# A fused attention and sparse-FFN kernel: x's split copy on ScalarE, the context's on GpSimd, P and out in one PSUM bank, and the attention phase unrolled

## The chip, the core and the metric

The kernel runs on one core of a Trainium2 chip. TensorE is called PE here, VectorE DVE, ScalarE ACT, GpSimd POOL and SyncE SP, as in the profile. The metric is the time of one execution on the device in microseconds (us), of which the median over several runs is taken. The profile comes from one more execution, recorded by the hardware profiler.

## The reference

The input x is (32, 64, 512), the context ctx (32, 64, 512). In the first half each of the 32 samples goes through a cross attention with linear cost, in the second all 2048 rows go through a sparse FFN:

```python
q = layernorm(x)                       # over the 512 columns
qh, kh, vh = Wq @ q, Wk @ ctx, Wv @ ctx        # 8 heads of 64, per sample
qh = softmax(qh, over the 64 rows of a head) / 8
kh = softmax(kh, over the 512 columns)
context = einsum('hdn,hen->hde', kh, vh)
out = Wo @ einsum('hde,hdn->hen', context, qh) + bo
x = x + out / norm(out) * g * 8
...
h = relu(x_ln @ w1.T) where it is the largest of its 32 by a rank-16 forecast, else 0
x = x + h @ w2t
```

The order of the products is changed in the kernel: with P = ctx E^T (64x512, E the exponentials of kh, not yet divided by their sums) and vo = Wv^T Wo^T per head (computed once), G = P^T vo, scaled by the sums, is the matrix that the softmaxed Q is multiplied with. So Wv and Wo cost little per sample.

## The kernel before

**Two phases.** `attention_phase` handles one sample per tile, 32 tiles, and writes the attention's output to a scratch tensor in HBM. `ffn_phase` then handles 16 tiles of two samples. The change touches the first phase alone.

**The pipeline.** Each engine has its own program, a sequence of steps g = -1 to 33, and the engines meet through semaphores alone; nothing plans the order but the order in which the lines stand. In step g three samples are in work at once: sample g+1 is prepared (layernorm, splits), sample g gets its K projection and later its Q projection, the E of sample g-1 is turned and multiplied with the context (P), and for sample g-2 Q is turned and multiplied with G (out). The condition `real(known, s)` says whether sample g+s exists. `steps` writes out the steps g = -1 to 4 and 29 to 33 and runs the 24 steps between in a loop of 12 rounds of two, in which the waits are for register values.

**The splits.** The two projections need more precision than one product in fp32r gives. Each input is loaded twice, into partitions 0 to 63 and 64 to 127. A copy rounds all 128 partitions to fp32r (x_split: DVE L352; c_split: ACT L411), and then POOL replaces the lower 64 by the remainder, value minus rounded value (x_split L247, c_split L251). A matmul over 128 partitions so sums the rounded part and the remainder. `x_ready` and `c_ready` count the finished splits; PE's projections wait for them (L507, L490), and SP waits for them before it loads the tile after next (L184, L186).

**PE's step** (L434 to L514): turn(0), that is four 128x128 transposes of E into turn_e and four of Q into turn_q; the 16 records of the G matmuls (L483), which need the copy of P from the step before; turn(1); products(0), which wait for G of DVE; the K projection; turn(2), products(1), turn(3), products(2), products(3); the Q projection. products(m) is one matmul of P (L471, PSUM bank pg, partitions 0 to 63) and one of out (L474, bank acc, partitions 64 to 127). turn_q waits for q_scaled, that is for POOL's L236.

**DVE's step** (L287 to L354): for each half of Q the maximum over a head (qmax) and the subtraction (L310), with G (L293) behind the first half; neg_kmax of the K projection, twice (L323); bn_stats and bn_aggr of x (L327, L329); twice the sum of Q's exponentials and its reciprocal (L333, L339); krec; the normalized x (xn, L347); its rounded copy (L352). In step 1 `split_ffn_constants` (L270) follows, on raw constants that lie in out_sb and Q.

**ACT's step** (L360 to L422): the copies of turn_e and turn_q to SBUF (ET, QT) and the exponentials in turn, then c_split's rounded copy (L411), the eviction of P (L414) and that of out with the bias bo (L421).

**POOL's step** (L209 to L253): the split of a slice of the FFN weights, 448 columns (L218, L220), which waits for c_ready; var_eps and rstd (L226, L229), which wait for the moments; the two multiplications of Q by its reciprocal sums (L236); the lower halves of x_split (L247) and c_split (L251).

## Time and profile before

| what | us |
|---|---|
| median of three runs (lowest, highest) | 937.48 (936.69, 938.23) |
| span of the profiled execution, first to last instruction | 936.1 |
| time of an execution around that span, median less span | 1.4 |
| PE busy | 845.2 (90%) |
| DVE busy | 723.7 (77%) |
| POOL busy | 426.4 (46%) |
| ACT busy | 404.7 (43%) |

The attention phase takes the span up to about 500 us, the FFN the rest. The shares are means over both phases, which load the engines differently, so the phase must be read by itself. The mean granted clock of TensorE over the span is 0.980 of full speed. A time in a timeline is a start, counted from the span's start, and the number behind it is how long the instruction (or the group, as x4 says) took; in brackets stands how long the engine had been idle before it and what ended that. Consecutive instructions of an engine overlap by some hundredths, so that a start to a start is the better measure of what one costs.

### The profile page before, as it was taken

How to read it: one execution, taken by the hardware profiler on the slowest of the kernel's cores; microseconds unless marked ns; L12 is line 12 of the kernel's file. 1: busy time of each engine (PE TensorE's matmuls, PEld its weight loads, DVE VectorE, ACT ScalarE, POOL GpSimd, SP SyncE). 2: the span in 40 equal slices, each digit the busy share in tenths (PEclk: the TensorE clock that was granted, in tenths of full speed). 3: DMA queues.
4: the chain of work that ended last, by engine and by line, in shares of the span. 5: the costliest groups of instructions: out<-in, count | busy, mean ns of one | idle time of the engine just before them, and what ended most of it. 6: DMA issues, size and time to landing. Idle time of an engine off the chain costs nothing. (4 is left out here: it accounts for less than half of the span.)

```text
span 936.1 us, 15499 instructions
## 1 busy us (share of the span) xinstructions
PE 845.2 (90%) x4752; PEld 599.4 (64%) x4752; DVE 723.7 (77%) x1020; ACT 404.7 (43%) x802; POOL 426.4 (46%) x422
## 2 busy tenths in 40 slices
PE   3679989899999899999994999999999999999998
PEld 2445555554555555555552788888888888888887
DVE  3989999999999999999971566666667666666664
ACT  2457777677777776776772111111111111111110
POOL 2635575665665755656640333333233333333322
PEclk9979999999999999999996799999999999999999
DMA  7212322312222222223002010110001010110000
GB/s 206 71 32 62 84 63 69 85 55 76 78 61 79 68 68 81 55 76 87 24 7 79 1 35 34 35 35 12 22 34 34 34 34 34 34 34 34 11 0 23
DMA packets 30200, 47.71 MB, mean 51 GB/s; under 512 B 4832, under 2 KB 13152, under 8 KB 30176
## 3 DMA queue, kind: packets, MB, share of 16 engines
q1 hardware_dynamic: 30176, 47.40, 17.3%
q8 instruction: 13, 0.21, 0.1%
q14 instruction: 11, 0.09, 0.0%
HBM read 39.00 MB, written 8.39 MB: 51 GB/s over the span
## 5 line engine op out<-in xcount | busy, mean ns | idle before, releaser
L471 PE MATMUL pg<-ET,ctxT 128*64 128x512 f32 x256 | 136.5, 616 | 40.9 <-DVE G L293 39.1
L626 POOL TENSOR_TENSOR ranked<-mask,rank 128x512 bf16<-128x512 bf16 x64 | 70.0, 1094 | 157.3 <-DVE mask L764 156.3
L236 POOL TENSOR_TENSOR Q<-Q,qrec 128x1024 f32<-128x1024 f32 x64 | 125.9, 1988 | 30.6 <-DVE qrec L339 30.6
L474 PE MATMUL acc<-QT,G 128*64 128x512 f32 x256 | 137.7, 621 | 0.0
L368 ACT ACTIVATE Q<-Q 128x1024 f32<-128x1024 f32 x64 | 67.8, 1059 | 74.1 <-DVE Q L310 74.1
L689 ACT ACTIVATE hT_hi<-turned 128x512 fp32r<-128x512 f32 x64 | 34.9, 545 | 149.4 <-PE turned L900 149.4
L390 ACT ACTIVATE ET<-turn_e 128x512 f32<-128x512 f32 x128 | 76.4, 597 | 49.9 <-PE turn_e L444 49.9
L890 PE MATMUL hidden<-weights_hi,xT_hi 128*128 128x512 f32 (+1 forms) x256 | 96.0, 375 | 0.0
L890 PE MATMUL hidden<-weights_hi,xT_lo 128*128 128x512 f32 (+1 forms) x256 | 94.8, 370 | 0.0
L890 PE MATMUL hidden<-weights_lo,xT_hi 128*128 128x512 f32 (+1 forms) x256 | 94.6, 370 | 0.0
L379 ACT ACTIVATE E<-slot,neg_kmax 128x512 f32<-128x512 f32 x128 | 88.0, 710 | 12.9 <-DVE neg_kmax L323 12.9
L913 PE MATMUL acc<-weights_hi,hT_hi 128*128 128x512 f32 x224 | 92.5, 413 | 0.0
L913 PE MATMUL acc<-weights_hi,hT_lo 128*128 128x512 f32 x224 | 88.0, 393 | 0.0
L913 PE MATMUL acc<-weights_lo,hT_hi 128*128 128x512 f32 x224 | 87.6, 391 | 0.0
L323 DVE TENSOR_REDUCE neg_kmax<-slot 128x2 f32<-128x1024 f32 x64 | 77.0, 1224 | 11.2 <-PE slot L498 8.1
L783 DVE SCALAR_TENSOR_TENSOR h_sb<-behind,hidden 128x512 f32<-128x512 bf16 x64 | 39.7, 621 | 58.0 <-POOL behind L635 36.4
L444 PEld LDWEIGHTS turn_e<-ident,E 128*128 128x128 f32 x512 | 59.1, 141 | 39.4 <-ACT ET L390 28.4
L452 PE MATMUL turn_q<-ident,Q 128*128 128x128 f32 x512 | 78.6, 276 | 5.8 <-POOL Q L236 4.4
L444 PE MATMUL turn_e<-ident,E 128*128 128x128 f32 x512 | 80.9, 281 | 1.2 <-ACT ET L390 1.2
L310 DVE TENSOR_TENSOR Q<-slot,qmax 128x1024 f32<-128x1024 f32 x64 | 78.3, 1224 | 4.5
L396 ACT ACTIVATE QT<-turn_q 128x512 f32<-128x512 f32 x128 | 76.8, 600 | 8.5 <-PE turn_q L452 6.5
L471 PEld LDWEIGHTS pg<-ET,ctxT 128*64 128x64 f32 x256 | 24.6, 135 | 85.6 <-issue 56.4
(96 smaller groups left out, 1894.3 us busy)
## 6 DMA issues: line engine op xcount, KB each, us to landing
x_in<-in_x SPq DMA_DIRECT2D x64, 128.0 KB, 2.6
c_in<-in_ctx SPq DMA_DIRECT2D x64, 128.0 KB, 2.7
stage<-in_ffn_w SPq DMA_DIRECT2D x32, 224.0 KB, 2.5
ctxT<-in_ctxT SPq DMA_DIRECT2D x32, 128.0 KB, 2.1
attn_out<-out_sb SPq DMA_DIRECT2D x32, 128.0 KB, 2.3
attn<-attn_out SPq DMA_DIRECT2D x16, 256.0 KB, 2.7
xr<-in_x SPq DMA_DIRECT2D x16, 256.0 KB, 2.9
out<-result SPq DMA_DIRECT2D x16, 256.0 KB, 2.0
```

What stands on the lines that cost most here:

```text
L236: nc.gpsimd.tensor_tensor(half, half, qrec[1 - par][:, s, :].unsqueeze(2).broadcast_to([P, HALF, D]), ALU.mult).then_inc(q_scaled, 1)
L310: nc.vector.tensor_tensor(heads(Q[1 - par][:, 2 * s:2 * s + 2, :]), src, qmax[:, s, :].unsqueeze(2).broadcast_to([P, HALF, D]), ALU.subtra ...
L323: nc.vector.tensor_reduce(neg_kmax[par][:, 2 * s:2 * s + 2], slot[s][:], AX.X, ALU.max, negate=True).then_inc(k_max, 1)
L379: last = nc.scalar.activation(E[par][:, j, :], slot[s][:, i, :], ACT.Exp, bias=neg_kmax[par][:, j:j + 1], accum_out=ksum[par][:, j:j + 1])
L390: nc.scalar.activation(ET[m % 2][:], turn_e[:], ACT.Copy).then_inc(e_copied, 1)
L396: nc.scalar.activation(QT[m % 2][:], turn_q[:], ACT.Copy).then_inc(q_copied, 1)
L444: last = nc.tensor.transpose(turn_e[:, j * P:(j + 1) * P], E[1 - par][:, j, m * P:(m + 1) * P], ident[:])
L452: last = nc.tensor.transpose(turn_q[:, t * P:(t + 1) * P], Q[par][:, t, m * P:(m + 1) * P], ident[:])
L471: nc.tensor.matmul(pg[0:C, :], ctxT[1 - par][:, m, :], ET[m % 2][:], start=(m == 0), stop=(m == NT - 1)).then_inc(p_mm, 1)
L474: nc.tensor.matmul(acc[C:P, :], G[par][:, m, :], QT[m % 2][:], start=(m == 0), stop=(m == HT - 1)).then_inc(out_mm, 1)
L890: last = nc.tensor.matmul(hidden[c % 2][:, 0:w], x[par][:, m, :], wt, start=(n == 0), stop=(n == len(terms) - 1))
L913: last = nc.tensor.matmul(acc[:], h[c % 2][:, cols], w2(wt, kt), start=(kt == 0 and n == 0), stop=(kt == KT - 1 and n == 2))
```

## The change

Four things change in the attention phase:

- DVE no longer makes the rounded copy of x. ACT does, as its last instruction of a step.
- ACT no longer makes the rounded copy of the context. POOL does, and its lower half follows at once; both now stand between rstd and the multiplications of Q, which wait for them (`c_ready`). x's lower half stays behind those multiplications.
- P and out go into one PSUM bank, po (P in partitions 0 to 63, out in 64 to 127), and one ACT instruction evicts both with a bias that is zero for P. G's matmuls use the other bank, gp. The raw FFN constants that lay in out_sb now lie in QT.
- The loop of 12 rounds is written out; all waits are for constants.

The diff, cut to what matters (renamings of tiles and semaphores left out):

```diff
--- before.py
+++ after.py
@@ -42,7 +42,6 @@
...
-FIRST_LOOPED, LAST_LOOPED = 5, B - 4
...
-def steps(eng, step):
-
-    for g in range(-1, FIRST_LOOPED):
-        step(g, g // 2, g % 2, g)
-    with eng.Fori(FIRST_LOOPED // 2, LAST_LOOPED // 2) as k:
-        step(2 * k + 1, k, 1, None)
-        step(2 * k + 2, k + 1, 0, None)
-    for g in range(LAST_LOOPED + 1, B + 2):
+def steps(step):
+
+    for g in range(-1, B + 2):
         step(g, g // 2, g % 2, g)
...
         ET = [sb(f"ET{i}", [P, HID]) for i in range(2)]
         QT = [sb(f"QT{i}", [P, N]) for i in range(2)]
-        PT = sb("PT", [C, HID])
         G = [sb(f"G{i}", [P, HT, C]) for i in range(2)]
-        out_sb = [sb(f"out_sb{i}", [P, N]) for i in range(2)]
-        c1_raw, rank_raw = out_sb[0][:], out_sb[1][:]
+        po_sb = [sb(f"po_sb{i}", [P, N]) for i in range(2)]
+        c1_raw, rank_raw = QT[0][:], QT[1][:]
...
-        pg = ps("pg", [P, 512])
-        acc = ps("acc", [P, 512])
+        po = ps("po", [P, 512])
+        gp = ps("gp", [P, 512])
...
@@ -193,10 +186,10 @@
                             sp.wait_ge(p_mm, NT * g)
                         load_ctxT(g + 1, 1 - par)
                     if real(known, -2):
-                        sp.wait_ge(out_copied, g - 1)
-                        sp.dma_start(scratch[g - 2], out_sb[par][C:P, :]).then_inc(stored[par], 16)
-
-                steps(sp, step)
+                        sp.wait_ge(po_copied, g)
+                        sp.dma_start(scratch[g - 2], po_sb[par][C:P, :]).then_inc(stored[par], 16)
+
+                steps(step)
...
             def _(pool):
                 nc.gpsimd.memset(neg_half[:], -0.5).then_inc(powers_set, 1)
                 nc.gpsimd.memset(eps[:], EPS).then_inc(powers_set, 1)
-                pool.wait_ge(powers_set, 2)
+                nc.gpsimd.memset(po_bias[0:C, :], 0.0).then_inc(powers_set, 1)
+                pool.wait_ge(powers_set, 3)
 
                 def step(g, k, par, known):
 
 
                     if later(g + 1 if known is None else min(g + 1, B)):
                         pool.wait_ge(c_ready, g + 1 if known is None else min(g + 1, B))
+                        pool.wait_ge(x_ready, g + 1 if known is None else min(g + 1, B))
...
@@ -228,8 +223,19 @@
                         pool.wait_ge(x_var, g + 2)
                         nc.gpsimd.tensor_tensor(rstd[1 - par][:], var_eps[:], neg_half[:],
                                                 ALU.pow).then_inc(x_rstd, 1)
+
+                        pool.wait_ge(c_loaded[1 - par], 32 * ((k if par == 0 else k + 1) + 1))
+                        if later(2 * g):
+                            pool.wait_ge(k_proj, 2 * g)
+                        nc.gpsimd.tensor_copy(c_split[1 - par][:], c_in[1 - par][:]).then_inc(c_hi, 1)
+                        pool.wait_ge(c_hi, g + 2)
+                        nc.gpsimd.tensor_tensor(c_split[1 - par][C:P, :], c_in[1 - par][C:P, :],
+                                                c_split[1 - par][C:P, :].bitcast(fp32),
+                                                ALU.subtract).then_inc(c_ready, 1)
                     if real(known, -1):
 
+                        if real(known, 1):
+                            pool.wait_ge(c_ready, g + 2)
                         for s in range(2):
                             pool.wait_ge(q_rec, 2 * g - 1 + s)
                             half = heads(Q[1 - par][:, 2 * s:2 * s + 2, :])
@@ -247,12 +253,8 @@
                         nc.gpsimd.tensor_tensor(x_split[1 - par][C:P, :], xn[C:P, :],
                                                 x_split[1 - par][C:P, :].bitcast(fp32),
                                                 ALU.subtract).then_inc(x_ready, 1)
-                        pool.wait_ge(c_hi, g + 2)
-                        nc.gpsimd.tensor_tensor(c_split[1 - par][C:P, :], c_in[1 - par][C:P, :],
-                                                c_split[1 - par][C:P, :].bitcast(fp32),
-                                                ALU.subtract).then_inc(c_ready, 1)
-
-                steps(pool, step)
+
+                steps(step)
...
@@ -346,14 +348,10 @@
                             dve.wait_ge(x_ready, g + 1)
                         nc.vector.tensor_scalar(xn[:], x_in[1 - par][:], moments[1 - par][:, 0:1],
                                                 rstd[1 - par][:], ALU.subtract, ALU.mult).then_inc(x_normed, 1)
-                        dve.wait_ge(x_normed, g + 2)
-                        if later(2 * g):
-                            dve.wait_ge(q_proj, 2 * g)
-                        nc.vector.tensor_copy(x_split[1 - par][:], xn[:]).then_inc(x_hi, 1)
                     if known == 1:
                         split_ffn_constants()
 
-                steps(dve, step)
+                steps(step)
...
@@ -390,6 +388,8 @@
                             nc.scalar.activation(ET[m % 2][:], turn_e[:], ACT.Copy).then_inc(e_copied, 1)
                         if real(known, -2):
                             use = HT * (g - 2) + m
+                            if known == 2 and m == 0:
+                                act.wait_ge(ffn_consts_done, 5)
                             act.wait_ge(q_turned, use + 1)
                             if later(use - 1):
                                 act.wait_ge(out_mm, use - 1)
...
@@ -403,31 +403,32 @@
                     exp_k(0)
                     copy(3)
                     exp_k(1)
+                    if real(known, -1) or real(known, -2):
+
+                        rows = slice(0 if real(known, -1) else C, P if real(known, -2) else C)
+                        if known == 1:
+                            act.wait_ge(powers_set, 3)
+                        if real(known, -1):
+                            act.wait_ge(p_mm, NT * g)
+                        if real(known, -2):
+                            act.wait_ge(out_mm, HT * (g - 1))
+                            if later(16 * (k - 1)):
+                                act.wait_ge(stored[par], 16 * (k - 1))
+                        nc.scalar.activation(po_sb[par][rows, :], po[rows, :], ACT.Identity,
+                                             bias=po_bias[rows, :]).then_inc(po_copied, 1)
                     if real(known, 1):
-
-                        act.wait_ge(c_loaded[1 - par], 32 * ((k if par == 0 else k + 1) + 1))
+                        act.wait_ge(x_normed, g + 2)
                         if later(2 * g):
-                            act.wait_ge(k_proj, 2 * g)
-                        nc.scalar.activation(c_split[1 - par][:], c_in[1 - par][:], ACT.Copy).then_inc(c_hi, 1)
-                    if real(known, -1):
-                        act.wait_ge(p_mm, NT * g)
-                        nc.scalar.activation(PT[:], pg[0:C, :], ACT.Copy).then_inc(p_copied, 1)
-                    if real(known, -2):
-                        if known == 2:
-                            act.wait_ge(ffn_consts_done, 5)
-                        act.wait_ge(out_mm, HT * (g - 1))
-                        if later(16 * (k - 1)):
-                            act.wait_ge(stored[par], 16 * (k - 1))
-                        nc.scalar.activation(out_sb[par][C:P, :], acc[C:P, :], ACT.Identity,
-                                             bias=bo[C:P, :]).then_inc(out_copied, 1)
-
-                steps(act, step)
+                            act.wait_ge(q_proj, 2 * g)
+                        nc.scalar.activation(x_split[1 - par][:], xn[:], ACT.Copy).then_inc(x_hi, 1)
+
+                steps(step)
...
@@ -459,29 +460,27 @@
                             pe.wait_ge(e_copied, NT * (g - 1) + m + 1)
                             if m == 0:
                                 pe.wait_ge(ctxT_loaded[1 - par], 16 * ((k - 1 if par == 0 else k) + 1))
-                                if later(g - 1):
-                                    pe.wait_ge(g_ready, g - 1)
                         if real(known, -2):
                             pe.wait_ge(q_copied, HT * (g - 2) + m + 1)
                             if m == 0:
                                 pe.wait_ge(g_ready, g - 1)
-                                if later(g - 2):
-                                    pe.wait_ge(out_copied, g - 2)
                         if real(known, -1):
-                            nc.tensor.matmul(pg[0:C, :], ctxT[1 - par][:, m, :], ET[m % 2][:],
+                            nc.tensor.matmul(po[0:C, :], ctxT[1 - par][:, m, :], ET[m % 2][:],
                                              start=(m == 0), stop=(m == NT - 1)).then_inc(p_mm, 1)
                         if real(known, -2):
-                            nc.tensor.matmul(acc[C:P, :], G[par][:, m, :], QT[m % 2][:],
+                            nc.tensor.matmul(po[C:P, :], G[par][:, m, :], QT[m % 2][:],
                                              start=(m == 0), stop=(m == HT - 1)).then_inc(out_mm, 1)
 
                     turn(0)
                     if real(known, -2):
                         pe.wait_ge(vo_ready, 1)
-                        pe.wait_ge(p_copied, g - 1)
+                        pe.wait_ge(po_copied, g - 1)
+                        if later(g - 2):
+                            pe.wait_ge(g_ready, g - 2)
                         for h in range(HEADS):
                             r = (h % 2) * D
-                            last = nc.tensor.matmul(pg[r:r + D, (h // 2) * C:(h // 2 + 1) * C],
-                                                    PT[:, h * D:(h + 1) * D], vo[:, h, :], start=True, stop=True)
+                            last = nc.tensor.matmul(gp[r:r + D, (h // 2) * C:(h // 2 + 1) * C],
+                                                    po_sb[1 - par][0:C, h * D:(h + 1) * D], vo[:, h, :], start=True, stop=True)
                         last.then_inc(g_mm, 1)
                     turn(1)
```

## Rows read from the trace of the kernel before

**Rows 1.** Windows view, 300 to 400 us: busy us (instructions) by engine, clock, DMA, GB/s.
```profile
300.00:400.00 100.00, 91.67 (x560) 53.70 (x558) 96.37 (x112) 74.34 (x147) 62.15 (x56) 1.00 0.25 70
```

**Rows 2.** Timeline of DVE, one step in the loop: start us, us, engine, line, operation.
```profile
302.84 0.18 DVE L329 BATCH_NORM_AGGREGATE moments<-stats 128x2 f32<-128x6 f32 x1
...
306.80 2.01 DVE L352 CAST x_split<-xn 128x512 fp32r<-128x512 f32 x1
...
317.20 0.18 DVE L329 BATCH_NORM_AGGREGATE moments<-stats 128x2 f32<-128x6 f32 x1
```

**Rows 3.** Timeline of DVE in unrolled steps, the first and the last.
```profile
59.18 0.18 DVE L329 BATCH_NORM_AGGREGATE moments<-stats 128x2 f32<-128x6 f32 x1
...
457.45 2.41 DVE L323 TENSOR_REDUCE neg_kmax<-slot 128x2 f32<-128x1024 f32 x2
...
460.55 0.18 DVE L329 BATCH_NORM_AGGREGATE moments<-stats 128x2 f32<-128x6 f32 x1
...
463.44 0.94 DVE L347 TENSOR_SCALAR xn<-x_in,moments,rstd 128x512 f32<-128x512 f32 x1
...
471.64 2.42 DVE L323 TENSOR_REDUCE neg_kmax<-slot 128x2 f32<-128x1024 f32 x2
```

**Rows 4.** Timeline of PE, 455 to 506 us, the same unrolled steps.
```profile
466.29 0.63 PE L452 MATMUL turn_q<-ident,Q 128*128 128x128 f32 x4
466.85 0.68 PE L483 MATMUL pg<-vo,PT 64*64 64x64 f32 x16
467.46 0.66 PE L444 MATMUL turn_e<-ident,E 128*128 128x128 f32 x4
467.96 0.60 PE L452 MATMUL turn_q<-ident,Q 128*128 128x128 f32 x4
469.40 0.61 PE L471 MATMUL pg<-ET,ctxT 128*64 128x512 f32 x1 [0.85 <-DVE G L293]
469.41 0.64 PE L474 MATMUL acc<-QT,G 128*64 128x512 f32 x1
469.86 0.59 PE L471 MATMUL pg<-ET,ctxT 128*64 128x512 f32 x1
```

**Rows 5.** Timelines of the start: DVE, POOL and PE.
```profile
13.66 0.43 DVE L352 CAST x_split<-xn 128x512 fp32r<-128x512 f32 x1
...
15.45 1.26 POOL L251 TENSOR_TENSOR c_split<-c_in,c_split 64x512 fp32r<-64x512 f32 x1
...
16.77 0.79 PE L497 MATMUL slot<-c_split,wk_hi 128*128 128x512 f32 x1 [6.38 <-POOL c_split L251]
```

**Rows 6.** Timeline of POOL, 455 to 500 us (unrolled steps).
```profile
460.81 0.19 POOL L226 TENSOR_TENSOR var_eps<-moments,eps 128x1 f32<-128x1 f32 x1 [4.07 <-DVE moments L329]
461.08 0.55 POOL L229 TENSOR_TENSOR rstd<-var_eps,neg_half 128x1 f32<-128x1 f32 x1
462.20 3.95 POOL L236 TENSOR_TENSOR Q<-Q,qrec 128x1024 f32<-128x1024 f32 x2 [0.57 <-DVE qrec L339]
466.60 1.26 POOL L247 TENSOR_TENSOR x_split<-xn,x_split 64x512 fp32r<-64x512 f32 x1 [0.45 <-DVE x_split L352]
467.82 1.27 POOL L251 TENSOR_TENSOR c_split<-c_in,c_split 64x512 fp32r<-64x512 f32 x1
469.16 0.56 POOL L218 CAST weights_hi<-stage 128x448 fp32r<-128x448 f32 x1
469.80 1.14 POOL L220 TENSOR_TENSOR weights_lo<-stage,weights_hi 128x448 fp32r<-128x448 f32 x1
475.55 3.76 POOL L236 TENSOR_TENSOR Q<-Q,qrec 128x1024 f32<-128x1024 f32 x2 [4.61 <-DVE qrec L339]
```

**Rows 7.** All instructions of line 218: ns minimum, median, maximum, first and last start.
```profile
L218 POOL CAST weights_hi<-stage x32: 556/556/635, 16.8 to 469.2; 128x448 f32 x24, 128x448 fp32r<-128x448 f32 x8
```

**Rows 8.** Groups of instructions, 100 to 500 us, on ACT: busy us, mean ns | idle before.
```profile
L421 ACT ACTIVATE out_sb<-acc,bo 64x512 f32<-64x512 f32 x29 | 19.8, 684 | 2.0 <-PE acc L474 1.3
L411 ACT ACTIVATE c_split<-c_in 128x512 fp32r<-128x512 f32 x26 | 17.7, 681 | 0.0
```

More of the change, by code:

```diff
@@ L79, in attention_phase @@
         vo = sb("vo", [C, HEADS, C])
-        bo = sb("bo", [P, 1])
+        po_bias = sb("po_bias", [P, 1])
         ident = shared["ident"]
@@ L135, in attention_phase @@
         q_sum, q_rec, q_scaled = sem("q_sum"), sem("q_rec"), sem("q_scaled")
-        e_turned, e_copied, p_mm, p_copied = sem("e_turned"), sem("e_copied"), sem("p_mm"), sem("p_copied")
-        q_turned, q_copied, out_mm, out_copied = sem("q_turned"), sem("q_copied"), sem("out_mm"), sem("out_copied")
+        e_turned, e_copied, p_mm, po_copied = sem("e_turned"), sem("e_copied"), sem("p_mm"), sem("po_copied")
+        q_turned, q_copied, out_mm = sem("q_turned"), sem("q_copied"), sem("out_mm")
         g_mm, g_ready = sem("g_mm"), sem("g_ready")
@@ L167, in _ @@
                 sp.dma_start(woT, A["woT"]).then_inc(consts_in, 16)
-                sp.dma_start(bo[C:P, :], A["bo"]).then_inc(consts_in, 16)
+                sp.dma_start(po_bias[C:P, :], A["bo"]).then_inc(consts_in, 16)
                 sp.dma_start(ident[:], A["ident"]).then_inc(consts_in, 16)
@@ L266, in prologue @@
                     dve.wait_ge(vo_mm, 1)
-                    nc.vector.tensor_copy(vo[:], acc[0:C, :].rearrange("c (h o) -> c h o", h=HEADS))\
+                    nc.vector.tensor_copy(vo[:], gp[0:C, :].rearrange("c (h o) -> c h o", h=HEADS))\
                         .then_inc(vo_ready, 1)
@@ L293, in gains @@
                             nc.vector.scalar_tensor_tensor(
-                                G[par][:], pg[:, 0:HT * C].rearrange("p (j o) -> p j o", j=HT), SCALE,
+                                G[par][:], gp[:, 0:HT * C].rearrange("p (j o) -> p j o", j=HT), SCALE,
                                 krec[:].unsqueeze(2).broadcast_to([P, HT, C]), ALU.mult, ALU.mult)\
@@ L429, in _ @@
                 for h in range(HEADS):
-                    last = nc.tensor.matmul(acc[0:C, h * C:(h + 1) * C], wv[:, h, :], woT[:, h, :],
+                    last = nc.tensor.matmul(gp[0:C, h * C:(h + 1) * C], wv[:, h, :], woT[:, h, :],
                                             start=True, stop=True)
@@ L514, in step @@
                             last.then_inc(q_proj, 1)
-                steps(pe, step)
+                steps(step)
 def ffn_phase(nc, A, shared, scratch, out):
```

## The prediction

> **What bounds the kernel now.** I read the page's shares first, then the windows by stage, then the timelines of DVE, PE and POOL for single steps. In the attention phase DVE is busy 96.4 of 100 us and PE 91.7 [rows 1]. Let A be the start of the moments instruction (L329), one per step. In the loop A comes back after 317.20 - 302.84 = 14.36 us [rows 2]; in the last unrolled step I get 471.64 - 457.45 = 14.19 from one neg_kmax to the next [rows 3]. From A at 59.18 to A at 460.55 there are 28 such intervals, 401.4 us, 14.33 each [rows 3]. DVE is the bound, and PE waits for it once a step, 0.85 us in front of L471, for G [rows 4]. The reader should see two more things.
>
> First, the removed cast L352 is not 2.01 us of work. At the start, where POOL is idle, it takes 0.43 us [rows 5], in a step 2.01 us [rows 2], because it is held while POOL runs its two Q multiplications (L236). POOL pays too: the two took 3.95 us with DVE's xn (L347, 463.44) among them, and 3.76 us at 475.55, where there is no xn [rows 3, 6].
>
> Second, a chain through POOL is hardly shorter than the step: A at 460.55, var_eps, rstd, Q multiplications to 462.20 + 3.95 = 466.15, turn_q(0) on PE at 466.29 [rows 3, 4, 6]. PE is released there by POOL and only then meets the wait for G. What enters that chain before L236 is paid as soon as it exceeds the 0.85 us.
>
> **The change part by part.** The removed DVE cast takes 2.01 us per step off the bound: 14.2 - 2.0 leaves DVE about 12.2 us. PE is busy 91.7% of 14.36, 13.2 us. So the bound would move to PE, if nothing else were in the way.
>
> The context split moves. Its low half L251 stood behind the Q multiplications, off the chain, in a stretch before POOL idled 4 us for the next moments [rows 6]. Now c_hi (new, a 128x512 copy) and the low half stand between rstd and L236 in every step, and L236 waits for both. I walk the chain once, from A = 0, in unrolled durations, since everything is unrolled now:
> - var_eps at +0.26, rstd 0.27 after it (460.55, 460.81, 461.08) [rows 3, 6]: 0.53.
> - rstd lasts 0.55; a ready POOL instruction starts 0.04 before its predecessor ends (466.60 + 1.26 against 467.82) [rows 6]: c_hi starts at 1.04.
> - c_hi is not in the trace. The nearest row is L218, the same copy with 448 columns: 0.556 us, at most 0.635 in 32 [rows 7]. By columns that is 0.64, at most 0.73; the low end is 0.56, and the far bound from above is the two-input low half, 1.27 [rows 6], since a copy reads less. I take 0.64, since L218 is the same operation and steady. The wait for its own result costs 0.08 (469.16 + 0.56 to 469.80): the low half starts at 1.76.
> - Low half 1.27, own wait 0.07 (467.82 + 1.27 to 469.16) [rows 6]: L236 may start at 3.10. Before, it started at 462.20 - 460.55 = 1.65.
> - Two Q multiplications. xn comes on DVE at 463.44 - 460.55 = 2.89, so it falls among them again: 3.95 [rows 3, 6]; 3.76 if it slips into the gap. Q is scaled at 7.05.
> - turn_q(0) came 0.14 after that (466.15 to 466.29) [rows 4, 6]; a PE that has long been waiting may need less, so I take 0.10 and 0.05 as the low end: 7.15.
> - turn_q(0) 0.56, G's matmuls 0.61, turn_e(1) 0.50, turn_q(1) 0.56 like the first: products(0) at 9.38 [rows 4]. G is there by then: DVE, freed of 2 us, has done the first qmax and shift and needs only G itself behind G's matmuls, while turn(1) runs. The 0.85 us wait is gone.
> - products(0) to neg_kmax: 469.40 to 471.64, 2.24 [rows 3, 4]: 11.62.
> - neg_kmax to A: 457.45 to 460.55, 3.10 [rows 3]. The step closes at 14.72.
>
> The second turn_q is a little generous (its end overlaps the next start), and so is 3.95 where a gap awaits xn; I take **14.66**. Low end, with c_hi 0.56, 3.76 and 0.05, each off the 14.66: about 14.35. High end, 14.72 with c_hi 0.73 and the full 0.14: 14.85.
>
> The steps: 28 x 14.66 = 410.5 against 401.4, **+9.1 us** (low +0.4, high +14.4). The last step's A to neg_kmax, 471.64 - 460.55 = 11.09 [rows 3], becomes 14.66 - 3.10 = 11.56: **+0.5**.
>
> The GPSIMD Engine Reference of the Trainium skill (section 4.1, Engine selection) speaks against this move: elementwise work belongs on VectorE, with GpSimd about twice as slow for two inputs and near line rate for one, and its Key points say twice as fast for VectorE without that distinction. By the general factor on the free cast's 0.43 us c_hi would be an estimated 0.86 and the total some 6 us above mine; L218's row sides with the distinction.
>
> The unrolling: the loop's 24 intervals take about 14.36 and the unrolled ones 14.19 [rows 2, 3], so 0.17 x 24 = 4 us would come back if DVE stayed the bound. My 14.66 is built from unrolled rows and holds it already.
>
> ACT swaps c_split for x_hi, of the same shape (0.68), and loses one of its two evictions (0.6 to 0.7) [rows 8], on an engine with a quarter of its time idle [rows 1]. x_hi is ready near A + 4.5; its low half on POOL can't start before 7.05, and then POOL has 14.66 - 7.05 = 7.6 us for 1.26 and the stage pair 0.64 + 1.14 [rows 6]. PE's q_proj needs x_ready most of a step later. Price nothing; without that cover it would be the 1.26 of a low half per step. SP waits for the same x_ready and c_ready before it loads the tiles after next, read a step later; c_ready comes earlier in a step than before, x_ready about 1.5 us later, both hidden.
>
> P and out share a bank: one eviction waits for both ends, which come together (L471 and L474 start 0.01 us apart [rows 4]). G's matmuls need it only after the next turn(0), when it is long done. Nothing.
>
> The start: PE's first projection was released at 16.77 by the low half of c, which stood behind that of x (15.45) [rows 5]. Now c's pair comes first: from rstd's end (DVE's cast at 13.66 [rows 5] came one xn of some 0.55 after it, so near 13.0) 0.64 + 0.3 for an xn in between + 1.27 gives 15.2. That is 1.5 us back, and the cast taken out ahead of DVE's ffn splits in the second step gives some tenths: **-2** (0 to -4). QT as staging makes ACT's first QT copy wait for those splits; the step's first qmax stands behind the same splits on DVE, and PE waits for G behind it anyway. The memset: nothing.
>
> **Sum.** 9.1 + 0.5 - 2.0 = +7.6. The profiled span is 936.1, so 943.7; the median of the runs lies 1.4 above that span, which gives **945.1 us**.
>
> **Rivals.**
> - The chain closes shorter, at 14.35 to 14.45: total 935 to 939. It needs c_hi at 0.56 and xn wholly in a gap. 0.17, of it 0.06 faster by over 0.2% and 0.11 within it.
> - DVE's relief reaches the end, the other side: POOL starts the pair in its 4 us of idling, ahead of the moments. It decides if Q is scaled before A + 5.7; then PE's 13.2 us set the step, 28 x (13.2 - 14.33) - 2 = -34: 903. For it: DVE and PE both have the room. Against: POOL issues in order, and var_eps, which needs the moments, stands ahead of the pair. 0.05.
> - POOL's copy is dearer, held by DVE's work beside it: from 0.73 up to the two-input 1.27, a step of 14.9 to 15.3, 951 to 963. Against: L218 is steady. The general factor of the Trainium skill, named above, lies in here. 0.06.
> - Matmuls of P and out, now in one bank, no longer overlap: four pairs of about 1 us, +4 us on PE, a step near 17, over 1000 us. Against: G's 16 matmuls write two halves of one bank within 0.61 us [rows 4], 0.04 each, where L471 moves 512 columns in two of 0.45, or 0.06 for 64 columns. 0.03.
> - PE's single wait, near 1.7 us now, makes the granted clock fall from 1.00 [rows 1]: 0.02.
>
> My forecast holds the remaining 0.67; its own range is 940 to 950. The range that should hold 8 in 10 reaches down over most of the short chain and up to the dear copy: **936 to 951**. A measurement tells a change from none at about 0.2%, 1.9 us: faster 0.11, same 0.12, slower 0.77.
>
> **What would show it.** In the profile after: A to A 14.6 to 14.7; DVE idle some 2 us per step in front of G and neg_kmax; PE's wait moved from L471 (G) to turn_q (POOL's Q); L236 released by c_ready, not by qrec; c_hi near 0.64. If PE still waits for G, or A to A is near 13.3, the chain is wrong; if L471 and L474 start 0.5 us apart, the bank is.

## The result: 3.2% slower, four times the loss that was forecast

The changed kernel takes 968.28 us (median of four runs, 964.25 to 969.62) against 937.62 before: a ratio of 1.0318, 95% interval 1.0295 to 1.0341, or +30.7 us. The forecast was +7.6 and a range up to 951.

The page of the changed kernel. Its profiled execution has a span of 967.1 us, 31.0 more than before.

```profile
span 967.1 us, 14352 instructions
...
PE 860.8 (89%) x4752; PEld 610.4 (63%) x4752; DVE 656.8 (68%) x988; ACT 390.0 (40%) x771; POOL 446.2 (46%) x455
...
PEclk9889999899999989999989599999999999999999
...
q8 instruction: 28, 0.46, 0.2%
q14 instruction: 24, 0.20, 0.1%
...
L468 PE MATMUL po<-ET,ctxT 128*64 128x512 f32 x256 | 148.9, 667 | 4.3 <-DVE G L295 1.2
...
L453 PE MATMUL turn_q<-ident,Q 128*128 128x128 f32 x512 | 85.3, 293 | 58.0 <-POOL Q L242 52.2
```

DVE lost 67 us of work and is no longer the bound. PE's idle time in front of the products (the row of L471 before) shrank from 40.9 to 4.3 us, and 58.0 us in front of turn_q (L453) took its place, 52.2 of them for POOL's Q multiplications. The line PEclk gives the granted clock in slices of 24 us, and some of those of the attention phase have an 8 where the others have a 9.

Where the 31 us are, from the moments instruction A of step 2 to that of step 30, as in [rows 3] (timeline of DVE):

```profile
58.17 0.18 DVE L331 BATCH_NORM_AGGREGATE moments<-stats 128x2 f32<-128x6 f32 x1
...
72.79 0.18 DVE L331 BATCH_NORM_AGGREGATE moments<-stats 128x2 f32<-128x6 f32 x1
```

The same view at the end of the 28 steps:

```profile
490.60 0.18 DVE L331 BATCH_NORM_AGGREGATE moments<-stats 128x2 f32<-128x6 f32 x1
...
503.77 2.35 DVE L325 TENSOR_REDUCE neg_kmax<-slot 128x2 f32<-128x1024 f32 x2 [1.83 <-PE slot L497]
```

The 28 steps take 490.60 - 58.17 = 432.4 us against 401.4, +31.0. The start gave 1.0 back (58.17 against 59.18), the last A to neg_kmax costs 503.77 - 490.60 = 13.17 against 11.09, +2.1, and what follows is 1.1 shorter. The sum is the 31.0 of the span.

The step from 58.17 to 72.79 takes 14.62 us; the forecast was 14.66. But only half of the steps are like it. Of the 28 intervals, 13 take 14.62 to 14.65 us, one 14.98, and 14 take 16.20 to 16.28. So +8.3 us come from 28 x (14.63 - 14.33), and 14 x 1.6 = 22.4 us from something that strikes every other step on average.

It is TensorE's clock. The timeline of PE in two steps of the changed kernel, a long one and a short one:

```profile
310.60 0.63 PE L453 MATMUL turn_q<-ident,Q 128*128 128x128 f32 x4 [1.61 <-POOL Q L242]
...
311.78 1.02 PE L445 MATMUL turn_e<-ident,E 128*128 128x128 f32 x4
...
313.58 1.12 PE L468 MATMUL po<-ET,ctxT 128*64 128x512 f32 x1
...
315.44 0.50 PE L496 MATMUL slot<-c_split,wk_hi 128*128 128x512 f32 x1
```

The short one, next to it:

```profile
326.88 0.63 PE L453 MATMUL turn_q<-ident,Q 128*128 128x128 f32 x4 [1.71 <-POOL Q L242]
...
328.05 0.66 PE L445 MATMUL turn_e<-ident,E 128*128 128x128 f32 x4
...
329.07 0.64 PE L468 MATMUL po<-ET,ctxT 128*64 128x512 f32 x1
...
330.08 0.50 PE L496 MATMUL slot<-c_split,wk_hi 128*128 128x512 f32 x1
```

In both PE waits for POOL's Q, 1.61 and 1.71 us. Then the same instructions take different times: from turn_e(1) to the K projection 315.44 - 311.78 = 3.66 us in the first, 330.08 - 328.05 = 2.03 in the second. Windows ahead of the slow part of the long step, in it and behind it show the cause in the clock column, the third from the right:

```profile
310.60:311.80 1.20, 1.20 (x21) 0.96 (x21) 0.00 (x0) 0.53 (x2) 1.11 (x1) 1.00 0.00 0
313.00:315.00 2.00, 2.00 (x8) 0.54 (x6) 1.74 (x2) 1.22 (x3) 0.85 (x1) 0.50 0.64 167
316.00:319.70 3.70, 3.70 (x22) 2.38 (x21) 2.96 (x3) 1.65 (x5) 0.00 (x0) 1.00 0.16 54
```

1.00 is 2.4 GHz and 0.50 the lower level, 1.2 GHz. PE had idled 1.61 us; the clock was still full for the first 1.2 us of work behind that wait and then fell. Over 60 to 490 us its mean is 0.94; the kernel before has 1.00 over the same stretch, with its longest wait at 0.84 to 1.01 us a step. Which of the changed kernel's steps is struck can't be read from the wait: PE idles 1.5 to 2.0 us for POOL in all of them, and the steps after a wait of 1.7 us were mostly spared, those after one of 1.6 us mostly struck.

The timeline of POOL in the long step:

```profile
303.69 0.19 POOL L221 TENSOR_TENSOR var_eps<-moments,eps 128x1 f32<-128x1 f32 x1 [4.45 <-DVE moments L331]
303.96 0.55 POOL L224 TENSOR_TENSOR rstd<-var_eps,neg_half 128x1 f32<-128x1 f32 x1
304.46 0.61 POOL L230 CAST c_split<-c_in 128x512 fp32r<-128x512 f32 x1
305.15 1.27 POOL L232 TENSOR_TENSOR c_split<-c_in,c_split 64x512 fp32r<-64x512 f32 x1
306.50 3.96 POOL L242 TENSOR_TENSOR Q<-Q,qrec 128x1024 f32<-128x1024 f32 x2
```

And that of DVE:

```profile
303.43 0.18 DVE L331 BATCH_NORM_AGGREGATE moments<-stats 128x2 f32<-128x6 f32 x1
...
306.32 0.52 DVE L349 TENSOR_SCALAR xn<-x_in,moments,rstd 128x512 f32<-128x512 f32 x1
...
311.96 0.42 DVE L295 SCALAR_TENSOR_TENSOR G<-gp,krec 128x256 f32<-128x256 f32 x1 [1.81 <-PE gp L482]
```

The pair (L230, L232) stands where the forecast put it, and the Q multiplications follow it at once. DVE waits 1.81 us before G, so it has the room that was forecast.

### The profile page after: what moved, and what is told of

It is laid out like the page before. It is cut to its first block and busy times, and to the rows that moved or that the text cites. A ratio compares the mean times of both kernels' runs of the same rounds, so it can differ in the third digit from the quotient of the medians.

```text
span 967.1 us, 14352 instructions
## 1 busy us (share of the span) xinstructions
PE 860.8 (89%) x4752; PEld 610.4 (63%) x4752; DVE 656.8 (68%) x988; ACT 390.0 (40%) x771; POOL 446.2 (46%) x455
## 5 line engine op out<-in xcount | busy, mean ns | idle before, releaser
L468 PE MATMUL po<-ET,ctxT 128*64 128x512 f32 x256 | 148.9, 667 | 4.3 <-DVE G L295 1.2
L471 PE MATMUL po<-QT,G 128*64 128x512 f32 x256 | 149.6, 670 | 0.0
L453 PE MATMUL turn_q<-ident,Q 128*128 128x128 f32 x512 | 85.3, 293 | 58.0 <-POOL Q L242 52.2
L453 PEld LDWEIGHTS turn_q<-ident,Q 128*128 128x128 f32 x512 | 63.9, 151 | 67.3 <-issue 56.3
L305 DVE TENSOR_REDUCE qmax<-slot 128x16 f32<-128x1024 f32 x64 | 78.0, 1219 | 24.2 <-PE slot L512 24.1
L221 POOL TENSOR_TENSOR var_eps<-moments,eps 128x1 f32<-128x1 f32 x32 | 6.1, 192 | 181.8 <-DVE moments L331 181.8
L445 PEld LDWEIGHTS turn_e<-ident,E 128*128 128x128 f32 x512 | 61.1, 145 | 39.4 <-ACT ET L388 28.3
L445 PE MATMUL turn_e<-ident,E 128*128 128x128 f32 x512 | 84.8, 290 | 1.2 <-ACT ET L388 1.2
```

What stands on the lines that cost most here:

```text
L305: nc.vector.tensor_reduce(qmax[:, s, :], src, AX.X, ALU.max).then_inc(q_max, 1)
L445: last = nc.tensor.transpose(turn_e[:, j * P:(j + 1) * P], E[1 - par][:, j, m * P:(m + 1) * P], ident[:])
L453: last = nc.tensor.transpose(turn_q[:, t * P:(t + 1) * P], Q[par][:, t, m * P:(m + 1) * P], ident[:])
L468: nc.tensor.matmul(po[0:C, :], ctxT[1 - par][:, m, :], ET[m % 2][:], start=(m == 0), stop=(m == NT - 1)).then_inc(p_mm, 1)
L471: nc.tensor.matmul(po[C:P, :], G[par][:, m, :], QT[m % 2][:], start=(m == 0), stop=(m == HT - 1)).then_inc(out_mm, 1)
```

## The experiments

The ratio and its 95% interval compare each kernel with the kernel before, run by turns with it on the same chip. Not all experiments ran on one chip; the medians of the kernel before lie between 937.5 and 938.9 us, so that a difference of 1 us between two experiments means nothing. Step times are A to A in the profile. The diffs leave lines out, the waits above all, where "..." stands.

**The pair behind the Q multiplications.** One thing is moved in the changed kernel:

```diff
                         nc.gpsimd.tensor_tensor(rstd[1 - par][:], ...).then_inc(x_rstd, 1)
...
-                        nc.gpsimd.tensor_copy(c_split[1 - par][:], c_in[1 - par][:]).then_inc(c_hi, 1)
-                        pool.wait_ge(c_hi, g + 2)
-                        nc.gpsimd.tensor_tensor(c_split[1 - par][C:P, :], ...).then_inc(c_ready, 1)
                     if real(known, -1):
-                        if real(known, 1):
-                            pool.wait_ge(c_ready, g + 2)
                         for s in range(2):
...
+                        nc.gpsimd.tensor_copy(c_split[1 - par][:], c_in[1 - par][:]).then_inc(c_hi, 1)
+                        pool.wait_ge(c_hi, g + 2)
+                        nc.gpsimd.tensor_tensor(c_split[1 - par][C:P, :], ...).then_inc(c_ready, 1)
                         pool.wait_ge(x_rstd, g + 2)
```

> The changed kernel with one thing moved: POOL makes the rounded copy and the low half of the context behind the two Q multiplications, ahead of x's low half. Theory 1 (the pair ahead of the Q multiplications lengthens the chain A, POOL, turn_q, K projection, neg_kmax to 14.62 us, and PE's wait of 1.6 to 2.2 us in it makes the granted clock fall): the chain is back at 14.62 - 1.4 = 13.2 us a step, PE's wait for the Q multiplications is under 0.5 us, no dips of the clock, 28 x (13.2 - 15.44) = -63 us against the changed kernel, near 905. Rival (the clock falls because of the shared bank or the unrolled program, not of the wait): steps near 13.2 where the clock is full but dips in half of them as before, 930 or more. Rival (DVE's relief is worth nothing): 933 as the unrolled kernel before.

Measured: 903.43 us, ratio 0.9627 (0.9610 to 0.9644). The window view from 60 to 440 us:

```profile
60.00:440.00 380.00, 371.39 (x2306) 221.95 (x2308) 343.38 (x431) 292.83 (x573) 273.12 (x259) 1.00 0.26 75
```

PE in front of turn_q, timeline:

```profile
314.80 0.63 PE L452 MATMUL turn_q<-ident,Q 128*128 128x128 f32 x4 [0.18 <-POOL Q L232]
```

A of step 2, timeline of DVE:

```profile
57.84 0.18 DVE L330 BATCH_NORM_AGGREGATE moments<-stats 128x2 f32<-128x6 f32 x1
```

And A of step 30:

```profile
427.93 0.18 DVE L330 BATCH_NORM_AGGREGATE moments<-stats 128x2 f32<-128x6 f32 x1
```

The steps take (427.93 - 57.84) / 28 = 13.22 us, the clock is 1.00 and PE busy for 371 of 380 us, with 0.18 us of waiting for POOL in this step. Bank sharing and the unrolled program are as in the changed kernel, so neither lowers the clock by itself. The place of two instructions on POOL is worth 65 us.

**Filling PE's wait.** The chain stays as long as it is, PE gets work that nobody uses:

```diff
                             pe.wait_ge(q_copied, HT * (g - 2) + m)
+                            if m == 0:
+                                for t in range(12):
+                                    nc.tensor.transpose(turn_q[:, (t % NT) * P:(t % NT + 1) * P],
+                                                        E[1 - par][:, t % HT, 0:P], ident[:])
                             pe.wait_ge(q_scaled, 2 * g - 2)
```

> The changed kernel with 12 more transposes of E on PE ahead of its wait for the Q multiplications; their results are overwritten. They fill some 1.5 of the 1.6 us in which PE idles, and the chain through POOL stays as it is. Theory 1: granted clock 1.00 from 60 to 490 us, every step 14.62 us, 28 x (14.62 - 15.44) = -23 us against the changed kernel, near 945, which is what was predicted for the change. Rival (the clock falls for another cause than the wait): 968 or more, since PE has more to do and the dips stay.

Measured: 945.54 us, ratio 1.0077 (1.0060 to 1.0095). The window view:

```profile
60.00:490.00 430.00, 420.51 (x2728) 266.49 (x2724) 337.86 (x441) 297.24 (x588) 276.77 (x260) 1.00 0.24 67
```

The filling and turn_q behind it, timeline of PE:

```profile
310.44 1.47 PE L453 MATMUL turn_q<-ident,E 128*128 128x128 f32 x12
312.13 0.66 PE L457 MATMUL turn_q<-ident,Q 128*128 128x128 f32 x4 [0.21 <-POOL Q L242]
```

The wait that is left is 0.21 us, the clock stays at 1.00, and the steps take 14.58 us on average ((465.62 - 57.35) / 28). More work on PE made the kernel 23 us faster than the changed one, and it landed on the time that the chain alone forecasts. That splits the loss of 31 us: about 8 from the chain, 23 from the clock.

**A third of the filling.** Four transposes instead of twelve:

```diff
-                                for t in range(12):
+                                for t in range(4):
```

> The changed kernel with 4 filling transposes (about 0.5 us) ahead of PE's wait instead of 12. The idle stretch left is some 1.1 us, as long as in the kernel with the low half alone ahead (1.06), where the granted clock stayed at 1.00. Theory 1 in the form that only the length of PE's idle stretch matters: no dips, 945. If the whole of the stretch has to be filled: dips in some of the steps, 950 to 965. Rival (filling does nothing, the 12 transposes worked otherwise): 968.

Measured: 944.77 us, ratio 1.0070 (1.0054 to 1.0085). The window view:

```profile
60.00:490.00 430.00, 395.02 (x2491) 240.56 (x2489) 338.70 (x442) 298.02 (x592) 278.56 (x262) 1.00 0.24 66
```

turn_q in the timeline of PE:

```profile
314.12 0.66 PE L457 MATMUL turn_q<-ident,Q 128*128 128x128 f32 x4 [1.10 <-POOL Q L242]
```

1.10 us of waiting are left, and the clock doesn't fall. So the wait needn't be filled, only shortened, by 0.5 us here.

**The low half alone ahead.** The context's rounded copy goes to ACT, as its first instruction of a step. POOL keeps the low half ahead of the Q multiplications, and to order it behind rstd it waits for rstd:

```diff
...
-                        nc.gpsimd.tensor_copy(c_split[1 - par][:], c_in[1 - par][:]).then_inc(c_hi, 1)
+                        pool.wait_ge(x_rstd, g + 2)
                         pool.wait_ge(c_hi, g + 2)
                         nc.gpsimd.tensor_tensor(c_split[1 - par][C:P, :], ...).then_inc(c_ready, 1)
...
+                        nc.scalar.activation(c_split[1 - par][:], c_in[1 - par][:], ACT.Copy).then_inc(c_hi, 1)
                     copy(0)
```

> The changed kernel with the context's rounded copy on ACT, as its first instruction of a step; the low half alone stays on POOL ahead of the Q multiplications. It takes c_hi's 0.61 + 0.08 us out of the chain and nothing else. Theory 1: a step without a dip is 14.62 - 0.69 = 13.93 us, and PE's wait shrinks from 1.61 to some 0.92 us, about the 0.85 (loop: 1.01) of the kernel before, at which the clock stayed full; so no dips, 401 - 28 x (14.33 - 13.93) = 390 us for the 28 steps, 925. If the shorter wait still lets the clock fall in half of the steps: 945. Rival (the clock's fall has nothing to do with the length of the wait): 945 or more.

Measured: 931.04 us, ratio 0.9911 (0.9888 to 0.9934), 6 us above the first expectation. The window view:

```profile
60.00:465.00 405.00, 371.47 (x2304) 221.50 (x2301) 365.88 (x433) 304.84 (x602) 257.93 (x230) 1.00 0.25 70
```

turn_q in the timeline of PE:

```profile
304.36 0.63 PE L455 MATMUL turn_q<-ident,Q 128*128 128x128 f32 x4 [1.06 <-POOL Q L239]
```

rstd and the low half, timeline of POOL:

```profile
312.70 0.55 POOL L224 TENSOR_TENSOR rstd<-var_eps,neg_half 128x1 f32<-128x1 f32 x1
313.33 1.27 POOL L229 TENSOR_TENSOR c_split<-c_in,c_split 64x512 fp32r<-64x512 f32 x1
```

The clock is full again at a wait of 1.06 us, shortened without any filling. The step is 14.06 us and not 13.93, because the low half starts 0.63 us behind rstd's start, where the ready c_hi of the changed kernel started 0.50 behind it (303.96, 304.46): the added wait for rstd costs 0.13, times 28 is 3.6 us of the 6.

**The unrolling alone**, the kernel before with its 24 looped steps written out:

```diff
-    for g in range(-1, FIRST_LOOPED):
-        step(g, g // 2, g % 2, g)
-    with eng.Fori(FIRST_LOOPED // 2, LAST_LOOPED // 2) as k:
-        step(2 * k + 1, k, 1, None)
-        step(2 * k + 2, k + 1, 0, None)
-    for g in range(LAST_LOOPED + 1, B + 2):
+    for g in range(-1, B + 2):
         step(g, g // 2, g % 2, g)
```

> The kernel before with its loop written out and nothing else. Both theories: DVE stays the bound, the 24 looped intervals of 14.36 us become 14.19, -4 us, 933.5. If the unrolled program stalls on fetching or lowers the clock, it is slower than before instead.

Measured: 935.27 us, ratio 0.9968 (0.9956 to 0.9980). Its 28 steps take 457.36 - 59.66 = 397.7 us, 3.7 less than before, at 14.18 each but for two of 14.53.

**Unrolled, with P and out merged, and nothing moved between engines.** On top of the edit above, the change's bank po and its one eviction replace the two, G's matmuls get the bank gp and the raw FFN constants lie in QT. The eviction:

```diff
-                        nc.scalar.activation(PT[:], pg[0:C, :], ACT.Copy).then_inc(p_copied, 1)
...
-                        nc.scalar.activation(out_sb[par][C:P, :], acc[C:P, :], ACT.Identity,
-                                             bias=bo[C:P, :]).then_inc(out_copied, 1)
...
+                        nc.scalar.activation(po_sb[par][rows, :], po[rows, :], ACT.Identity,
+                                             bias=po_bias[rows, :]).then_inc(po_copied, 1)
```

> The kernel before, unrolled, with P and out in one bank and one eviction; x's rounded copy stays on DVE, the context's on ACT, its low half behind x's. Theory 1: DVE stays the bound at 14.19 us, ACT's saving is off the path, so 933.5 as unrolled alone, within 2. Rival (the shared bank costs PE something or lowers its clock): 940 or more, with dips of the clock or products longer than 1.02 us.

Measured: 934.29 us, ratio 0.9958 (0.9943 to 0.9974), steps of 14.18 us, clock 1.00. The shared bank and the single eviction cost nothing and bring nothing that these runs can tell.

**x's copy back on DVE**, in the changed kernel:

```diff
+                        nc.vector.tensor_copy(x_split[1 - par][:], xn[:]).then_inc(x_hi, 1)
...
-                        nc.scalar.activation(x_split[1 - par][:], xn[:], ACT.Copy).then_inc(x_hi, 1)
```

> The changed kernel with x's rounded copy back on DVE, behind xn. Theory 1 (the chain through POOL sets the step, DVE has slack): DVE idles 1.8 us in front of G and 0.8 in front of qmax, so the copy, which gets in between the two Q multiplications and ends near A + 5.3, costs nothing. Steps 14.62 without a dip of the clock, 16.2 with one, PE's wait for the Q multiplications as in the changed kernel: 968, within 4. Rival (DVE's relief is still worth part of its 2 us a step): 14.62 + 1.9 less the idle time, up to 28 x 1 us more, 990 or above.

Measured: 980.32 us, ratio 1.0445 (1.0418 to 1.0471). Neither theory had this. The timeline of POOL:

```profile
314.37 4.13 POOL L242 TENSOR_TENSOR Q<-Q,qrec 128x1024 f32<-128x1024 f32 x2
```

That of DVE:

```profile
314.73 2.01 DVE L354 CAST x_split<-xn 128x512 fp32r<-128x512 f32 x1
```

And the window view:

```profile
60.00:500.00 440.00, 384.54 (x2227) 227.57 (x2226) 373.85 (x445) 268.71 (x528) 270.48 (x251) 0.93 0.23 64
```

DVE had room for the copy, but POOL had not. The copy is held for 2.01 us as before, and where xn alone made the two Q multiplications 3.96 us long, xn and the copy make them 4.13. POOL is the chain, so an undisturbed step is 14.82 us and PE waits 1.7 to 1.9, at times 2.3. That is 5 us of the 12; the steps with the slow clock are 17 of 28 now, which is 5 more; and A of step 2 comes 1.3 us later, which is within what the start varies by between these kernels (57.35 to 59.52).

**x's copy on ACT alone**, in the kernel before, with its loop and its two evictions:

```diff
-                        nc.vector.tensor_copy(x_split[1 - par][:], xn[:]).then_inc(x_hi, 1)
...
                                              bias=bo[C:P, :]).then_inc(out_copied, 1)
+                        nc.scalar.activation(x_split[1 - par][:], xn[:], ACT.Copy).then_inc(x_hi, 1)
```

> The kernel before, loop and evictions as they were, with one part of the change alone: x's rounded copy moves from DVE to the end of ACT's step. The context's copy stays on ACT, its low half behind x's on POOL. Theory 1: DVE's relief reaches the end here, since nothing was put into the chain. The step becomes the chain of 13.2 us, plus some 0.1 to 0.2 for the loop's register waits: 13.3 to 13.4, 28 x -1 = -28 us, 908 to 911. Rival (the context's copy had to leave ACT to make room, ACT now carries both): ACT's step or x_hi is late, 920 or more.

Measured: 904.38 us, ratio 0.9629 (0.9609 to 0.9649). A of step 2, timeline of DVE:

```profile
58.65 0.18 DVE L329 BATCH_NORM_AGGREGATE moments<-stats 128x2 f32<-128x6 f32 x1
```

And of step 30:

```profile
429.01 0.18 DVE L329 BATCH_NORM_AGGREGATE moments<-stats 128x2 f32<-128x6 f32 x1
```

13.23 us a step. One of the four parts, put alone into the kernel before, makes it 34 us faster. ACT carries both rounded copies and both evictions without being late, so the context's copy did not have to leave it. The time is 4 us below the expectation, which had priced the loop's register waits at 0.1 to 0.2 us a step: the loop, worth 3.7 us while DVE was the bound, costs next to nothing here (13.22 us in the unrolled kernel with the pair behind, which differs in other parts too).

**DVE's moments ahead of G.** The next two experiments ask what sets the 13.2 us. The reading was: the chain neg_kmax, moments, qsum, Q multiplications, turn_q. In the kernel with the pair behind, bn_stats and bn_aggr move to where DVE waited for G:

```diff
                                 ALU.subtract).then_inc(q_shifted, 1)
                             if s == 0:
+                                statistics()
                                 gains()
```

> The kernel with the pair behind the Q multiplications (903.4 us), and bn_stats and bn_aggr moved on DVE from behind neg_kmax to the place between the first half of Q and G, where DVE idled 0.75 us. Theory: it takes 0.86 us out of the chain neg_kmax, moments, qsum, Q multiplications, turn_q; PE's waits of 0.18 to 0.55 us for them vanish, G is up to 0.15 us later but not late. PE is then the bound with 97.8% of 13.21 us busy: steps 12.8 to 13.0, 28 x -0.3 = -8, 892 to 898. Rival (PE's small waits are then for ACT's QT and ET copies instead): no change, 903.

Measured: 913.45 us, ratio 0.9727 (0.9707 to 0.9747), 10 us slower than the kernel it is made from; neither theory had this. The waits from 100 to 400 us (us in total, times, longest):

```profile
DVE qmax L311 <- PE slot L516: 29.1, 22, 1.3
...
PEld slot L500 <- DVE Q L318: 11.7, 22, 0.6
PE po L472 <- DVE G L301: 9.4, 22, 0.4
```

PE's wait for POOL is gone, as meant. In its place PE waits 0.43 us a step for G, and the K projection's weight load 0.53 for DVE's second subtraction (11.7 and 9.4 us over 22 steps), and DVE in turn waits 1.3 us a step for the Q projection (29.1 over 22 steps), which comes later for both: 13.59 us a step. I read from this that DVE's work from qmax to the second subtraction is a second chain, from the Q projection to the K projection, and that what looked like idle time in front of G was the slack of that chain. The next experiment, which leaves that place free, agrees.

**The moments a step ahead.** They are computed for the sample after the next at the end of DVE's step, where DVE waited for the Q projection:

```diff
-                    if real(known, 1):
...
-                        nc.vector.bn_stats(stats[:], x_in[1 - par][:])
...
-                        nc.vector.bn_aggr(moments[1 - par][:], stats[:]).then_inc(x_moments, 1)
...
+                    if real(known, 2):
+                        statistics(g + 2, par, k + 2)
```

> The kernel with the pair behind the Q multiplications (903.4 us), and DVE's bn_stats and bn_aggr for the next sample but one at the end of its step, behind xn, where it idled 0.4 us before qmax, instead of behind neg_kmax. That takes 0.86 us out of the chain neg_kmax, moments, qsum, Q multiplications, and unlike the placing ahead of G puts at most 0.46 us ahead of qmax, with G's idle 0.75 us to take it up. Theory: PE becomes the bound at 12.8 to 12.9 us a step, 28 x -0.36 = -10, 893. Rival (what is put ahead of qmax reaches PE through G and the K projection, as with the placing ahead of G): 903 or more.

Measured: 891.79 us, ratio 0.9514 (0.9498 to 0.9530), the fastest of all. The window view by hundreds:

```profile
200.00:300.00 100.00, 99.31 (x630) 60.92 (x629) 93.31 (x116) 78.24 (x155) 73.41 (x71) 1.00 0.29 83
```

12.82 us a step, PE busy for 99 of 100 us. That is PE's own time, and the end of what the order of the other engines' work can give. So the 13.2 us of the two kernels above were the chain's and not PE's.

## Why the prediction was wrong

**The chain was right, link by link.** From A, forecast and measured (303.43 the A of the rows above): c_hi starts at 1.04 and 1.03, takes 0.64 and 0.61; the Q multiplications start at 3.10 and 3.07; Q is scaled at 7.05 and 7.03; turn_q(0) starts at 7.15 and 7.17; products(0), in the undisturbed step, 2.23 and 2.19 later (326.88 to 329.07). The step closes at 14.66 and 14.62. The wait for G is gone, and DVE idles 1.81 us before G. The experiment with the pair behind shows that nothing but their place makes the chain: without the 3.10 - 1.65 = 1.45 us that they put ahead of the Q multiplications, 14.66 leaves 13.21, and 13.22 was measured. That the prediction also gave PE 13.2 us a step is a coincidence. It counted PE's busy time in a step, and with the moments a step ahead PE needs 12.82.

**The step that failed is the last rival**, "PE's single wait, near 1.7 us now, makes the granted clock fall from 1.00: 0.02". The wait was forecast to 0.1 us; its consequence was given two in a hundred and no price, and the walk along the chain took everything on PE behind the wait at the full clock. From turn_q(0) to neg_kmax the forecast has 2.23 + 2.24 = 4.47 us. The short step takes 331.31 - 326.88 = 4.43 and the long one 316.68 - 310.60 = 6.08 (timeline of DVE):

```profile
316.68 2.36 DVE L325 TENSOR_REDUCE neg_kmax<-slot 128x2 f32<-128x1024 f32 x2 [1.90 <-PE slot L497]
...
331.31 2.36 DVE L325 TENSOR_REDUCE neg_kmax<-slot 128x2 f32<-128x1024 f32 x2 [0.26 <-PE slot L497]
```

Rows for such a price were at hand in the kernel before: in step 2 PE idles 10.68 us for G, which stands behind DVE's split of the FFN constants, and then runs the same matmuls at a granted clock of 0.50, the products in 1.09 us and the first one of the K projection in 0.80, where in a step they take 0.61 (469.40 in [rows 4]) and 0.50. The timeline of PE and the window there:

```profile
51.58 1.09 PE L471 MATMUL pg<-ET,ctxT 128*64 128x512 f32 x1 [10.68 <-DVE G L293]
...
53.48 0.80 PE L497 MATMUL slot<-c_split,wk_hi 128*128 128x512 f32 x1
```

```profile
52.00:54.00 2.00, 2.00 (x5) 0.50 (x2) 1.73 (x2) 1.31 (x4) 0.00 (x0) 0.50 0.00 0
```

They give the price, not the chance: how short a wait is enough, no row of that kernel told, since its waits in the 28 steps are of 1 us and less, at 1.00. What the wait does in the changed kernel is shown by filling it: the same chain, the same program, 12 transposes more, and the time falls from 968.3 to 945.5, 0.4 us off the forecast of 945.1. Four transposes do the same. The term that was missing is 14 x 1.6 = 22.4 us; in the last step, from A to neg_kmax, it strikes once more, which makes the 0.5 us forecast there 2.1. Why only half of the steps are struck stays open.

**The minor terms.** The start was forecast at -2 and gave -1.0, although the first constants came 1.45 us later in this execution than in the one before (DVE's first cast at 9.86 against 8.41). With the same start the kernels with 12 and with four transposes reach A of step 2 at 57.35 and 59.32, so a single profile doesn't tell such a term to a microsecond. The unrolling, forecast at 4 us while DVE is the bound, gives 3.7 in the steps and 2.7 in the medians. ACT, SP and the shared bank cost nothing, as argued; P's and out's matmuls start together as in [rows 4].

**One reading was wrong.** The prediction put the 3.95 us of the two Q multiplications, against 3.76, down to xn among them. In that row the cast of x runs beside them as well, and taking the cast away doesn't shorten them: with x's copy on ACT alone they still take 3.95. So in the old order xn and the cast cost POOL together no more than xn alone. In the changed kernel it is different, since xn starts there 0.18 us ahead of the multiplications: with the cast back on DVE they take 4.13 instead of 3.96 and the step is 0.19 us longer, 5 of the 12 us that this experiment lost. The forecast's 3.95 was right for the changed kernel, by this luck.

**The sum by parts.** x's copy off DVE: -34 us, alone. The context's pair ahead of the Q multiplications: +65 us, of which 28 x (14.63 - 13.22) = 39.5 are the chain and 15 x 1.6 = 24 its effect on the clock, the last step included. Unrolling and merging: -3 or so while DVE is the bound, about nothing later. The change put the price of its second part on top of the gain of its first, which is why the net +30.7 looks like a small loss of a large change.

## What to carry to other kernels

When work moves to another engine, its place in that engine's order is a decision of its own: ask which chain passes there in every step. The same two instructions cost 65 us ahead of two multiplications and nothing behind them. And when a forecast makes PE wait longer in one piece, put a price on the lower clock next to the wait itself. Here the chain exceeded the old bound by 8 us in all, and the clock, lowered behind the wait it left, took 22 more in the 28 steps. A kernel's own slow stretches show what the lower clock costs it.

Before moving work into the idle time of an engine, walk the chain that ends that idle time. DVE's idle time in front of G was another chain's slack, and the 0.86 us of work put there cost 10 us; put in front of qmax it gained 12.

## What the runs showed of the chip

- The granted clock fell from 1.00 in 14 of 28 steps where PE had idled 1.5 to 2.0 us for POOL (the changed kernel), and in 17 of 28 where it had idled 1.7 to 2.3 (x's copy back on DVE). It stayed at 1.00 where PE idled 0.84 to 1.11 (before, the low half ahead, four transposes), the longest single wait in these being 1.5. A step it struck was 1.6 us longer. Each cure shortened the single wait and PE's idle time in the step alike, so the runs don't tell which of the two counts.
- DVE's work from SBUF to SBUF and POOL's instructions hold each other up. xn takes 0.52 us when it starts 0.18 us ahead of the two Q multiplications (306.32, 306.50), 0.94 when it starts 1.24 us into them [rows 3, 6], and 1.81 when it starts 0.38 us into them (the low half alone ahead, 315.06 against 314.68 on POOL). The pair of multiplications takes 3.76 us alone [rows 6], 3.94 to 3.96 with xn, 3.95 with xn and the cast in the order of the kernel before and 4.13 in that of the changed one. The GPSIMD Engine Reference of the Trainium skill (section 1, Specifications) says that POOL's interfaces to SBUF are shared with VectorE, and contended by VectorE's instructions in a two-port mode or with two inputs in SBUF. These rows agree that the two contend and give the price; in which mode xn and the cast run they don't show.
- In eight of the ten unrolled kernels one or two steps of the 28 are 0.35 us longer (14.98 against 14.63, 14.53 against 14.18); in the two with the moments moved, and in the two with the loop, none is. The trace of the low half ahead shows DVE idle for 0.43 us in such a step with nothing to wait for that the profile shows. The instruction queues moved 52 packets, 0.66 MB, in the changed kernel, against 24 and 0.30 before. That fetching is the cause is likely and wasn't tested.
